# Window-attention and FFN layer on eight cores: transposing the attention matrix behind the V projection instead of ahead of it

## The chip, the cores and the metric

The kernel runs on the 8 cores of one Trainium2 chip. Every core computes 2 of the 16 sequences by itself, with all weights, and no core waits for another. The metric is the device time of the slowest core in microseconds (us).

## The reference

Attention here is over channels: for a window of 256 tokens and one head the 64 x 64 matrix q k^T (summed over the 256 tokens) goes through a softmax and is applied to v. Windows overlap by half (`step = 128`). Only the first 4096 rows of the joined windows are kept, which are those of windows 0 to 15 of a sequence.

```python
qkv = (xp @ W_qkv + b_qkv).reshape(B, Lp, 3, HEADS, HEAD_DIM)
...
attn = jnp.einsum('bhndw,bhnew->bhnde', qw, kw) * HEAD_DIM ** (-0.5)
attn = jax.nn.softmax(attn, axis=-1)
o = jnp.einsum('bhnde,bhnew->bhndw', attn, vw)
o = o.reshape(B, HEADS, -1, HEAD_DIM)
o = o.transpose(0, 2, 1, 3).reshape(B, -1, C)
o = o[:, :L]
return o @ W_out + b_out
...
x = _layernorm(x + attention(x)); x = _layernorm(x + ffn(x))
ffn(x) = (silu(x wg^T) * (x wu^T)) wd^T
```

Shapes: x 16 x 4096 x 1024, 16 heads of 64, hidden size 3072. The three FFN weights come as integers times 1/127.

## The kernel before

The program has two phases. Phase A does the attention and the first layer norm, and beside that turns and rescales the FFN weights. Phase B is the FFN with the second layer norm. The change touches phase A alone.

Phase A goes over the 2 sequences `s` and in each over 18 steps `t` (0 to 17). A step works on two windows that are one step apart, and on one block of 128 tokens. All of the order is that in which Python emits the code: each engine runs its instructions in that order, and there is no scheduler. A step of the middle (`t` from 2 to 16) emits, in this order:

- `prep_loads(2)` and `emit_xload(gt + 3)`: DMAs of two blocks of FFN weight and one block of x, issued by GpSimd.
- `emit_qkv_pass(0)` and `(1)`: TensorE multiplies the token block `x_fm` into q and k (18 matmuls of 512 columns each pass, lines 522 to 534, in `psum_qkv`), and VectorE copies the two halves out (lines 555 and 558).
- The first part of window n1 = t - 1: TensorE makes the 64 x 64 products of 16 heads in `psum_S` (line 587, 32 matmuls); VectorE takes the row maximum off (lines 599 and 605, `ssub`).
- The transposes of the softmax result of window n = t - 2: TensorE transposes `a_bd` into the first quarter of `psum_O` (lines 625 and 628, 16 of them), and VectorE copies that to `at_bf` (line 638).
- `emit_qkv_pass(2)`: v, in the same way, into `v_tmp`.
- `emit_xtr(gt + 2)`: the next x block transposed (8, line 287) and copied out (line 296).
- v transposed (8, line 662) and copied to `v_fm` (line 671).
- `flush_typf(which=1)`: the first normalised row block of the window before, `y_bf`, transposed (8, line 320) and copied out (line 334).
- The attention output: TensorE multiplies `v_fm` with `at_bf` into `psum_O` (line 693, 64 matmuls). It waits for the copy of line 638.
- `flush_typf(which=2)`: the second row block `y_bf`, the same.
- `prep_trs(2)`: two blocks of FFN weight (`w_in_bf`) are rescaled by VectorE (line 399), transposed by TensorE (line 413), copied to `wT_stage` (line 423) and stored by a DMA. In the last jobs (`wd`) a block has three such batches. There are 56 jobs, so the last steps of sequence 1 have none.
- The output projection: ScalarE copies the attention output to `attn_out` (line 781), TensorE multiplies it with `wout_bf` (lines 727 to 739, two row blocks), VectorE adds x from a DMA (`xr`, line 750, `y1pre`). ScalarE then does the exponential of window n1 (line 790) and the layer norm (lines 799 to 834), and VectorE the row sums and the block-diagonal form `a_bd` of window n1 (lines 843 to 865).

The transposes write to one of three banks in turn, `psum_TR`, `psum_S` and `psum_qkv`, given out by `claim_tr()`. Step t = 17 has no q, k and v and no new window: it only finishes the last one. In step 16 of sequence 1 `emit_wg_stream` issues one DMA of 6144 KB (`wgT`) on SyncE's queue, which also carries the `xr` loads.

Of the waits two matter here: the wait of the attention output for the copy, and VectorE's copy itself, which waits for its own last instruction as well:

```python
b.wait(v, "V", at_mm_done[gw])
b.wait(v, "V", b.tok("V"))
b.wait(v, "V", o_mm_done.get(gw - 1))
...
b.wait(t_, "T", atevac_done[gw])
b.wait(t_, "T", tv_done[s * TB + n])
b.wait(t_, "T", tv_done[s * TB + n + 1])
```

Of the kernel before, what the change touches and what calls it, by code (L numbers as in the profile page):

```python
# [9 lines left out]
BF16 = mybir.dt.bfloat16  # L10
# [10 lines left out]
TB = 17  # L21
NW = 16
# [38 lines left out]
def build_program(debug=False, seqs=SEQS, l=L):  # L61
    TB = l // 256 + 1
    NW = l // 256
# [30 lines left out]
    b = Bld(nc, es_outer)  # L94
# [14 lines left out]
    psum_O = PS("psum_O", [128, 2048], F32)  # L109
# [11 lines left out]
    ident_sb = SA("ident_sb", [128, 128], BF16)  # L121
# [16 lines left out]
    a_bd = SA("a_bd", [128, 2, 8, 128], BF16)  # L138
    at_bf = SA("at_bf", [128, 1024], BF16)
# [22 lines left out]
    with nc.Block() as blk:  # L162
        @blk.gpsimd
        def _(g):
            b.inc(g.memset(ones128[:, :], 1.0), "G", 1)
            b.inc(g.memset(ones1[:, :], 1.0), "G", 1)
            b.inc(g.memset(a_bd[:, :, :, :], 0.0), "G", 1)
            b.inc(g.memset(lneps[:, :], float(EPS)), "G", 1)
# [76 lines left out]
    s_mm_done, ssub_done, exp_done, scale_done, bd_done = {}, {}, {}, {}, {}  # L245
    at_mm_done, atevac_done, o_mm_done, oevac_done = {}, {}, {}, {}
    proj_done, resid_done, sq_done, apply_done = {}, {}, {}, {}
# [5 lines left out]
    with nc.Block() as blk:  # L253
# [52 lines left out]
        def emit_ty_one(gw, s, n, k2):  # L306
            wsl = n % 4
            if True:
                grt = s * RTS + 2 * n + k2
                rsl = grt % 2  # L310
                bk, qtok = claim_tr()
                bi, freetok = bk[0], bk[1]

                @blk.tensor
                def _(t_, grt=grt, rsl=rsl, bi=bi, freetok=freetok, qtok=qtok):
                    b.wait(t_, "T", apply_done[grt])
                    b.wait(t_, "T", freetok)
                    b.wait(t_, "T", qtok)
                    for c in range(8):
                        b.inc(t_.transpose(tr_slice(bi, 128 * c, 128 * (c + 1)),  # L320
                                           y1_bf[:, rsl, 128 * c:128 * (c + 1)],
                                           ident_sb[:, :]), "T", 1)
                tymm_done[grt] = b.tok("T")

                pp1 = pf_by_idx.get(pf_idx[0] - 1)
                pp2 = pf_by_idx.get(pf_idx[0] - 2)

                @blk.vector
                def _(v, grt=grt, rsl=rsl, k2=k2, wsl=wsl, bi=bi, pp1=pp1, pp2=pp2):
                    b.wait(v, "V", tymm_done[grt])  # L330
                    b.wait(v, "V", pp1)
                    b.wait(v, "V", pp2)
                    dst = y1fm_stage[:, wsl, :, 128 * k2:128 * (k2 + 1)]
                    b.inc(v.tensor_copy(dst, tr_slice(bi, 0, 1024)
                                        .rearrange("p (a b) -> p a b", a=8)),
                          "V", 1)
                ty_done[grt] = b.tok("V")
                bk[1] = ty_done[grt]

        def emit_pf(gw, s, n):  # L340
            wsl = n % 4
            nw0 = n - wsl
            pi = pf_idx[0]
            pf_idx[0] += 1
            prev2 = pf_by_idx.get(pi - 2)

            @blk.gpsimd
            def _(g, s=s, n=n, gw=gw, wsl=wsl, nw0=nw0, pi=pi, prev2=prev2):
                b.wait(g, "G", prev2)
                b.wait(g, "G", ty_done[s * RTS + 2 * n])  # L350
                b.wait(g, "G", ty_done[s * RTS + 2 * n + 1])
                src_ap = y1fm_stage[:, 0:wsl + 1, :, :].rearrange(
                    "p w a b -> p w (a b)")
                b.inc(g.dma_start(
                    y1fm_h.ap()[s, nw0:n + 1].rearrange(
                        "w p a b -> p w (a b)"),
                    src_ap), "pf%d" % (pi % 2), 16)
            pf_done[gw] = b.tok("pf%d" % (pi % 2))
            pf_by_idx[pi] = pf_done[gw]

        def flush_typf(which=2):
            if pending_typf[0] is not None:
                gw0, s0, n0 = pending_typf[0]
                if which >= 1 and pending_typf[0] not in ty_started:
                    ty_started.add(pending_typf[0])
                    emit_ty_one(gw0, s0, n0, 0)
                if which == 2:
                    emit_ty_one(gw0, s0, n0, 1)
                    if (n0 % 4 == 3) or (n0 == NW - 1):
                        emit_pf(gw0, s0, n0)  # L370
                    pending_typf[0] = None
# [124 lines left out]
        for s in range(SEQSv):  # L496
            for t in range(TB + 1):
# [5 lines left out]
                have_w2 = t >= 2  # L503
# [104 lines left out]
                    ssub_done[gw1] = b.tok("V")  # L608
                    tr_banks[1][1] = ssub_done[gw1]

                if have_w2:
                    n = t - 2
                    gw = s * NW + n
                    sl0 = (s * TB + n) % 3
                    sl1 = (s * TB + n + 1) % 3
                    wpar = gw % 2

                    @blk.tensor
                    def _(t_, gw=gw, wpar=wpar):
                        b.wait(t_, "T", bd_done[gw])  # L620
                        b.wait(t_, "T", oevac_done.get(gw - 1))
                        b.wait(t_, "T", resid_done.get(2 * (gw - 1)))
                        at_dst = psum_O[:, 0:512].bitcast(BF16)
                        for hp in range(8):
                            b.inc(t_.transpose(at_dst[0:64, 128 * hp:128 * (hp + 1)],
                                               a_bd[:, wpar, hp, 0:64], ident_sb[:, :]),
                                  "T", 1)
                            b.inc(t_.transpose(at_dst[64:128, 128 * hp:128 * (hp + 1)],
                                               a_bd[:, wpar, hp, 64:128], ident_sb[:, :]),
                                  "T", 1)  # L630
                    at_mm_done[gw] = b.tok("T")

                    @blk.vector
                    def _(v, gw=gw):
                        b.wait(v, "V", at_mm_done[gw])
                        b.wait(v, "V", b.tok("V"))
                        b.wait(v, "V", o_mm_done.get(gw - 1))
                        b.inc(v.tensor_copy(at_bf[:, :], psum_O[:, 0:512].bitcast(BF16)),
                              "V", 1)
                    atevac_done[gw] = b.tok("V")  # L640

                if have_qkv:
                    emit_qkv_pass(2)
                    qkv_free[0] = evac_half[((gt, 2), 1)]
# [29 lines left out]
                    vbk[1] = tv_done[gt]  # L674

                if have_w2:
                    flush_typf(which=1)

                    @blk.tensor
                    def _(t_, gw=gw, s=s, n=n, sl0=sl0, sl1=sl1):  # L680
# [248 lines left out]
    with nc.Block() as blk:  # L929
# [77 lines left out]
        for g in range(NGg):  # L1007
            s = g // (Lv // 256)
# [237 lines left out]
```

How the kernel before makes its waits and increments, by code:

```python
    def inc(self, instr, name, by=1):  # L40
        instr.then_inc(self.sems[name], by)
        self.cnt[name] += by
        return (name, self.cnt[name])
# [4 lines left out]
    def wait(self, eng, engkey, tok):  # L48
        if tok is None:
            return
        name, val = tok
        if val <= 0:
            return
        key = (engkey, name)
        if self.waited.get(key, 0) >= val:
            return
        self.waited[key] = val
        eng.wait_ge(self.sems[name], val)
# [1153 lines left out]
        @blk.gpsimd  # L1212
        def _(g_):
            g_.wait_ge(b.sems["st0"], b.cnt["st0"])
            g_.wait_ge(b.sems["st1"], b.cnt["st1"])
```

## Time and profile before

| | us |
|---|---|
| median of 3 runs | 3558.66 |
| lowest and highest of them | 3373.44, 3881.48 |
| the profiled execution | 3367.28 |
| its span on the slowest core (core 3) | 3365.7 |
| spans of the eight cores | 3352.1 to 3365.7 |
| TensorE busy in the span | 2947.0 (88%) |
| VectorE, ScalarE, GpSimd busy | 935.4, 1248.5, 182.8 |

The profiled execution is one run of the program with the hardware profiler on, and its span is the time from the first to the last instruction of its slowest core. The times of the rows are counted from the start of that span. A row of the timeline is: start, duration, engine, line of the source, operation, what is written from what, and in square brackets how long the engine had been idle and what ended that. PE is TensorE, DVE is VectorE, ACT is ScalarE, POOL is GpSimd, SP is SyncE. "PEclk" is the clock granted to TensorE as a share of 2.4 GHz, so 0.50 is 1.2 GHz.

### The profile page before, as it was taken

To read this page: it belongs to the slowest core of one execution; us is meant where nothing else is said; L and a number is where in the kernel's file an instruction comes from. 1 tells how busy PE (TensorE), PEld (TensorE's weight loads), DVE (VectorE), ACT (ScalarE), POOL (GpSimd) and SP (SyncE) were. 2 spreads that over 40 slices of the span, in tenths; PEclk is the share of its full clock that TensorE was granted. 3 is DMA by queue.
4 is the path that set the end of the run, shared out by engine and by line. 5 is a ranking of instruction groups with operands and counts; after the bars stand their busy time and mean duration, and the time that the engine had idled before them with its cause. 6 is when DMAs were issued, how large, how long until landed. Compare 5 with 4: busy or idle time off the path is not lost.

```text
span 3365.7 us, 61503 instructions; the slowest of 8 cores (3352.1 to 3365.7 us)
## 1 busy us (share of the span) xinstructions
PE 2947.0 (88%) x23572; PEld 1985.5 (59%) x23572; DVE 935.4 (28%) x1750; ACT 1248.5 (37%) x2721; POOL 182.8 (5%) x324
## 2 busy tenths in 40 slices
PE   0888888788866764999999999999999999999997
PEld 0344444344433432777777777777777777777775
DVE  0344444344434431112212212212212222222221
ACT  0245454525434443223333323323323323323333
POOL 1011111101111100000000000000000000000000
PEclk9999999899988886999999999999999999999998
DMA  7234434324444344401101101101101111101100
GB/s 124 50 99 132 123 107 121 110 85 110 122 129 119 113 139 146 132 32 51 45 32 51 45 32 51 45 32 51 45 32 51 45 33 50 45 35 48 45 32 26
DMA packets 77216, 245.71 MB, mean 73 GB/s; under 512 B 8576, under 2 KB 8576, under 8 KB 76928
## 3 DMA queue, kind: packets, MB, share of 16 engines
q0 software_dynamic: 43744, 138.96, 14.3%
q1 hardware_dynamic: 33184, 102.81, 9.2%
q8 instruction: 193, 3.16, 0.4%
q14 instruction: 95, 0.78, 0.1%
HBM read 175.16 MB, written 102.76 MB: 83 GB/s over the span
## 4 chain that ended last, share of the span: by engine, by line
PE 60%; ACT 0%; DMA 0%; DVE 0%; issue 0%; SPq 0%; POOL 0%; ACTq 0%; DVEq 0%; POOLq 0%
PE psum_qkv L1044 20%; PE psum_O L1025 10%; PE psum_S L1054 10%; PE psum_TR L1054 10%; PE psum_O L1029 10%; DMA wuT<-wuT_scr 0%; DVE y2pre L1099 0%; ACT y L1209 0%; ACT y2sq L1189 0%; ACT y2sq L1192 0%; SPq L989 0%; ACT L1189 0%; SPq L981 0%; DVE h_bf L1075 0%; ACT l2ln L1205 0%
## 5 line engine op out<-in xcount | busy, mean ns | idle before, releaser
L1044 PE MATMUL psum_qkv<-y1fm_sb,wgT 128*128 128x256 bf16 x6144 | 797.8, 273 | 19.6 <-DMA y1fm_sb<-y1fm_scr 19.6
L1044 PEld LDWEIGHTS psum_qkv<-y1fm_sb,wgT 128*128 128x128 bf16 x6144 | 601.8, 98 | 247.0 <-issue 19.8
L1139 ACT ACTIVATE sg_bf<-psum_qkv 128x256 bf16<-128x256 f32 x768 | 293.7, 382 | 1188.2 <-PE psum_S L1054 672.3
L1025 PE MATMUL psum_O<-wdT,h_bf 128*128 128x512 bf16 x1536 | 581.9, 379 | 0.6 <-DVE h_bf L1075 0.6
L1029 PE MATMUL psum_O<-wdT,h_bf 128*128 128x512 bf16 x1536 | 582.0, 379 | 0.0
L1054 PE MATMUL psum_S<-y1fm_sb,wuT 128*128 128x256 bf16 x3072 | 399.0, 273 | 6.8 <-DMA wuT<-wuT_scr 6.8
L1054 PE MATMUL psum_TR<-y1fm_sb,wuT 128*128 128x256 bf16 x3072 | 398.1, 273 | 0.0
L1075 DVE TENSOR_TENSOR h_bf<-psum_TR,sg_bf 128x256 bf16<-128x256 f32 x384 | 163.2, 425 | 794.3 <-PE psum_O L1025 675.1
L1075 DVE TENSOR_TENSOR h_bf<-psum_S,sg_bf 128x256 bf16<-128x256 f32 x384 | 163.2, 425 | 759.6 <-PE psum_O L1025 717.4
L522 PE MATMUL psum_qkv<-wqkv_bf,x_fm 128*128 128x512 bf16 x816 | 315.3, 386 | 48.5 <-DVE q_tm L555 43.4
L1054 PEld LDWEIGHTS psum_S<-y1fm_sb,wuT 128*128 128x128 bf16 x3072 | 300.8, 98 | 42.3 <-issue 7.3
L527 PE MATMUL psum_qkv<-wqkv_bf,x_fm 128*128 128x512 bf16 x816 | 314.7, 386 | 7.6 <-DVE q_tm L558 7.1
L1054 PEld LDWEIGHTS psum_TR<-y1fm_sb,wuT 128*128 128x128 bf16 x3072 | 300.6, 98 | 34.8
L727 PE MATMUL psum_O<-wout_bf,attn_out 128*128 128x512 bf16 x512 | 220.1, 430 | 8.4 <-ACT attn_out L781 8.4
L1025 PEld LDWEIGHTS psum_O<-wdT,h_bf 128*128 128x128 bf16 x1536 | 150.0, 98 | 119.8 <-issue 21.2
L732 PE MATMUL psum_O<-wout_bf,attn_out 128*128 128x512 bf16 x512 | 217.4, 425 | 0.5 <-ACT attn_out L781 0.5
L1029 PEld LDWEIGHTS psum_O<-wdT,h_bf 128*128 128x128 bf16 x1536 | 150.0, 98 | 98.8
L799 ACT ACTIVATE y1sq<-y1pre 128x1024 f32<-128x1024 f32 x64 | 67.6, 1057 | 301.6 <-DVE y1pre L750 298.4
L522 PEld LDWEIGHTS psum_qkv<-wqkv_bf,x_fm 128*128 128x128 bf16 x816 | 80.7, 99 | 155.9 <-issue 72.4
L527 PEld LDWEIGHTS psum_qkv<-wqkv_bf,x_fm 128*128 128x128 bf16 x816 | 80.9, 99 | 109.2 <-issue 24.4
L1126 POOL DMA_DIRECT2D out<-y x64 | 34.1, 533 | 2018.3 <-ACT y L1173 1860.2
L781 ACT ACT_TABLE_LOAD x32 | 41.1, 1283 | 252.0 <-PE psum_S L320 133.1
(145 smaller groups left out, 2424.1 us busy)
## 6 DMA issues: line engine op xcount, KB each, us to landing
xr<-x SPq DMA_DIRECT2D x64, 512.0 KB, 3.5
y1dbg<-y_f POOLq DMA_DIRECT2D x64, 512.0 KB, 3.0
y1r<-y1dbg SPq DMA_DIRECT2D x64, 512.0 KB, 4.2
out<-y POOLq DMA_DIRECT2D x64, 512.0 KB, 2.9
y1fm_scr<-y1fm_stage POOLq DMA_DIRECT2D x8, 2048.0 KB, 7.7
y1fm_sb<-y1fm_scr SPq DMA_DIRECT2D x32, 512.0 KB, 4.6
xt_bf<-x POOLq DMA_DIRECT2D x34, 256.0 KB, 7.7
wqkv_bf<-wqkv POOLq DMA_DIRECT2D x8, 768.0 KB, 27.9
```

The costliest lines, as they stand in the source:

```text
L522: b.inc(t_.matmul(psum_qkv[:, 0:512], lhsT, wqkv_bf[:, c, 1024 * p:1024 * p + 512], start=(c == 0), stop=False), "T", 1)
L527: b.inc(t_.matmul(psum_qkv[:, 512:1024], lhsT, wqkv_bf[:, c, 1024 * p + 512:1024 * (p + 1)], start=(c == 0), stop=False), "T", 1)
L727: b.inc(t_.matmul(pj[:, 0:512], lhsT, wout_bf[:, c, 0:512], start=(c == 0), stop=False, skip_group_check=True), "T", 1)
L732: b.inc(t_.matmul(pj[:, 512:1024], lhsT, wout_bf[:, c, 512:1024], start=(c == 0), stop=False, skip_group_check=True), "T", 1)
L781: b.inc(a.activation(attn_out[:, hp, rb:rb + 256] .rearrange("p (d c) -> p d c", c=4), psum_O[:, base:base + 256] .rearrange("p (c d) -> p ...
L799: b.inc(a.activation(y1sq[:, :], y1pre[:, rsl, :], AF.Identity, accum_out=sums[:, rsl, :]), "A", 1)
L1025: b.inc(t_.matmul(down_ps[:, 1024 * rs:1024 * rs + 512], lhsT, wdT[:, hc, 0:512], start=(hc == 0), stop=(hc == 23), skip_group_check=True) ...
L1029: b.inc(t_.matmul(down_ps[:, 1024 * rs + 512:1024 * (rs + 1)], lhsT, wdT[:, hc, 512:1024], start=(hc == 0), stop=(hc == 23), skip_group_ch ...
L1044: b.inc(t_.matmul(gate_ps[hsl], wgT[:, hc, 128 * dc:128 * (dc + 1)], y1fm_sb[:, gsl, dc, :], start=(dc == 0), stop=(dc == 7)), "T", 1)
L1054: b.inc(t_.matmul(up_ps[hsl], wuT[:, hc, 128 * dc:128 * (dc + 1)], y1fm_sb[:, gsl, dc, :], start=(dc == 0), stop=(dc == 7)), "T", 1)
L1075: b.inc(v.tensor_tensor(h_bf[:, hsl, :], up_ps[hsl], sg_bf[:, hsl, :], ALU.mult), "V", 1)
L1139: b.inc(a.activation(sg_bf[:, hsl, :], gate_ps[hsl], AF.Silu), "A", 1)
```

## The change

In every step the 16 transposes of `a_bd` and VectorE's copy to `at_bf` are emitted later: behind the v pass, the x transposes, the v transposes and the first `y_bf` transposes, right ahead of the attention output. Nothing is added or taken away; the waits are the same ones. In the source the blocks of v move up instead, which is the same order:

```diff
@@ -608,12 +608,48 @@
                     tr_banks[1][1] = ssub_done[gw1]
 
+                if have_qkv:
+                    emit_qkv_pass(2)
+                    qkv_free[0] = evac_half[((gt, 2), 1)]
+                    emit_xtr(gt + 2)
+
+                if s == SEQSv - 1 and t == TB - 1 and wprep_tr[0] >= 24:
+                    emit_wg_stream(gt)
+
+                if have_qkv:
+                    vbk, vqtok = claim_tr()
...
                 if have_w2:
                     n = t - 2
                     gw = s * NW + n
                     sl0 = (s * TB + n) % 3
                     sl1 = (s * TB + n + 1) % 3
                     wpar = gw % 2
+
+                    flush_typf(which=1)
 
                     @blk.tensor
                     def _(t_, gw=gw, wpar=wpar):
@@ -638,43 +674,6 @@
                     atevac_done[gw] = b.tok("V")
-
-                if have_qkv:
-                    emit_qkv_pass(2)
...
-                if have_w2:
-                    flush_typf(which=1)
 
                     @blk.tensor
                     def _(t_, gw=gw, s=s, n=n, sl0=sl0, sl1=sl1):
```

From line 608 on the line numbers change: the transposes are lines 661 and 664 (625 and 628 before), their copy is 674 (638), the v transposes are 631 (662) and their copy 640 (671), and what stands behind them is one line earlier (the attention output 692, the projection 726 and 731).

TensorE, step 3 of sequence 0, behind the q k products. Before:

```order
L576 UNCONDITIONAL_BRANCH
L587 MATMUL psum_S<-k_tm,q_tm 64x64 x32
L618 UNCONDITIONAL_BRANCH
L625 MATMUL psum_O<-ident_sb,a_bd 64x128
L628 MATMUL psum_O<-ident_sb,a_bd 64x128
```

After, the same place:

```order
L576 UNCONDITIONAL_BRANCH
L587 MATMUL psum_S<-k_tm,q_tm 64x64 x32
L515 UNCONDITIONAL_BRANCH
L522 MATMUL psum_qkv<-wqkv_bf,x_fm 128x512
L527 MATMUL psum_qkv<-wqkv_bf,x_fm 128x512
```

The v pass now follows the products at once. TensorE around the attention output (`psum_O<-at_bf,v_fm`), the same step. Before:

```order
L287 MATMUL psum_S<-ident_sb,xt_bf 128x128 x8
L654 UNCONDITIONAL_BRANCH
L662 MATMUL psum_qkv<-ident_sb,v_tmp 128x128 x8
L314 UNCONDITIONAL_BRANCH
L320 MATMUL psum_TR<-ident_sb,y_bf 128x128 x8
L679 UNCONDITIONAL_BRANCH
L693 MATMUL psum_O<-at_bf,v_fm 64x64 x64
```

After, what stands ahead of the attention output (the two rows of the transposes come eight times each; the last pair is shown):

```order
L661 MATMUL psum_O<-ident_sb,a_bd 64x128
L664 MATMUL psum_O<-ident_sb,a_bd 64x128
L678 UNCONDITIONAL_BRANCH
L692 MATMUL psum_O<-at_bf,v_fm 64x64 x64
L314 UNCONDITIONAL_BRANCH
L320 MATMUL psum_S<-ident_sb,y_bf 128x128 x8
```

The 16 transposes moved from behind the q k products to the place right ahead of the attention output. VectorE, the same step, from the row maximum to the second `y_bf` copy. Before:

```order
L599 TENSOR_REDUCE negmax<-psum_S 128x8
L605 TENSOR_TENSOR ssub<-psum_S,negmax 128x512
L633 UNCONDITIONAL_BRANCH
L638 COPY at_bf<-psum_O 128x1024
L542 UNCONDITIONAL_BRANCH
L555 CAST v_tmp<-psum_qkv 128x512
L558 CAST v_tmp<-psum_qkv 128x512
L292 UNCONDITIONAL_BRANCH
L296 COPY x_fm<-psum_S 128x1024
L667 UNCONDITIONAL_BRANCH
L671 COPY v_fm<-psum_qkv 128x1024
```

After, from the v copies on:

```order
L555 CAST v_tmp<-psum_qkv 128x512
L558 CAST v_tmp<-psum_qkv 128x512
L292 UNCONDITIONAL_BRANCH
L296 COPY x_fm<-psum_S 128x1024
L636 UNCONDITIONAL_BRANCH
L640 COPY v_fm<-psum_qkv 128x1024
L328 UNCONDITIONAL_BRANCH
L334 COPY y1fm_stage<-psum_TR 128x8x128
L669 UNCONDITIONAL_BRANCH
L674 COPY at_bf<-psum_O 128x1024
L328 UNCONDITIONAL_BRANCH
L334 COPY y1fm_stage<-psum_S 128x8x128
```

The copy to `at_bf` moved behind five other copies. ScalarE, GpSimd and SyncE keep their order.

## Rows read from the trace of the kernel before

**Rows 1.** The page, its head and the first row of part 1.

```profile
span 3365.7 us, 61503 instructions; the slowest of 8 cores (3352.1 to 3365.7 us)
...
PE 2947.0 (88%) x23572; PEld 1985.5 (59%) x23572; DVE 935.4 (28%) x1750; ACT 1248.5 (37%) x2721; POOL 182.8 (5%) x324
```

**Rows 2.** Windows, PE alone: stretch, length, busy, PEclk, DMA share, GB/s.

```profile
162.70:599.90 437.20, 354.99 (x3250) 0.96 0.40 117
330.30:364.20 33.90, 27.60 (x250) 0.95 0.36 102
364.20:396.40 32.20, 25.91 (x250) 1.00 0.39 107
...
1318.00:3365.00 2047.00, 2015.24 (x15360) 0.99 0.14 48
```

**Rows 3.** Timeline of one step (t = 2 of sequence 1), TensorE.

```profile
700.52 0.45 PE L587 MATMUL psum_S<-k_tm,q_tm 128*64 128x64 bf16 x16 [0.73 <-DVE k_tm L555]
...
701.79 0.22 PE L628 MATMUL psum_O<-ident_sb,a_bd 128*64 128x128 bf16 x1
...
705.41 0.38 PE L530 MATMUL psum_qkv<-bq_rep,ones 128*128 128x512 bf16 x1
...
707.55 0.61 PE L320 MATMUL psum_qkv<-ident_sb,y_bf 128*128 128x128 bf16 x8
...
708.09 1.52 PE L693 MATMUL psum_O<-at_bf,v_fm 128*64 128x64 bf16 x64
...
712.01 0.61 PE L413 MATMUL psum_S<-ident_sb,w_in_bf 128*128 128x128 bf16 x8 [1.84 <-DVE w_in_bf L399]
```

**Rows 4.** The same timeline, VectorE and ScalarE.

```profile
701.99 0.69 DVE L599 TENSOR_REDUCE negmax<-psum_S 128x8 f32<-128x512 f32 x1 [1.02 <-PE psum_O L628]
...
702.79 0.69 DVE L605 TENSOR_TENSOR ssub<-psum_S,negmax 128x512 f32<-128x512 f32 x1
...
703.58 0.69 DVE L638 COPY at_bf<-psum_O 128x1024 bf16<-128x1024 bf16 x1
...
705.89 0.69 DVE L555 CAST v_tmp<-psum_qkv 128x512 bf16<-128x512 f32 x1 [1.62 <-PE psum_qkv L530]
...
708.42 0.68 DVE L334 COPY y1fm_stage<-psum_qkv 128x1024 bf16<-128x1024 bf16 x1
...
710.54 1.28 ACT L781 ACT_TABLE_LOAD   x1 [24.58 <-PE psum_TR L320]
710.84 0.69 DVE L334 COPY y1fm_stage<-psum_TR 128x1024 bf16<-128x1024 bf16 x1 [1.73 <-PE psum_TR L320]
```

**Rows 5.** Timeline of the step ahead (t = 1, without `a_bd` transposes), TensorE.

```profile
680.99 0.45 PE L587 MATMUL psum_S<-k_tm,q_tm 128*64 128x64 bf16 x16 [0.73 <-DVE k_tm L555]
...
685.43 0.38 PE L530 MATMUL psum_qkv<-bq_rep,ones 128*128 128x512 bf16 x1
```

**Rows 6.** Timeline, TensorE and VectorE, where something other holds the step.

```profile
636.70 1.01 PE L320 MATMUL psum_qkv<-ident_sb,y_bf 128*128 128x128 bf16 x8 [4.79 <-ACT y_bf L834]
...
993.05 0.69 DVE L423 COPY wT_stage<-psum_qkv 128x1024 bf16<-128x1024 bf16 x1 [10.84 <-DMA wdT_scr<-wT_stage]
...
1041.46 0.69 DVE L423 COPY wT_stage<-psum_TR 128x1024 bf16<-128x1024 bf16 x1 [4.34 <-DMA wdT_scr<-wT_stage]
...
1252.76 2.55 DVE L750 TENSOR_TENSOR y1pre<-psum_O,xr 128x1024 f32<-128x1024 f32 x2 [19.89 <-DMA xr<-x]
...
1262.56 1.92 PE L693 MATMUL psum_O<-at_bf,v_fm 128*64 128x64 bf16 x64
```

**Rows 7.** Windows again, PE alone: two steps of sequence 1, and a pause.

```profile
801.20:833.20 32.00, 26.08 (x250) 1.00 0.40 108
934.20:968.70 34.50, 28.60 (x250) 0.90 0.43 115
...
978.00:986.00 8.00, 1.86 (x31) 1.00 1.02 213
```

More of the change, by code:

```diff
@@ L609, in build_program @@
                     tr_banks[1][1] = ssub_done[gw1]
-                if have_w2:
[L612 to L640, printed above, removed]
                 if have_qkv:
@@ L676, in build_program, with _ @@
                 if have_w2:
-                    flush_typf(which=1)
+                    n = t - 2
+                    gw = s * NW + n
+                    sl0 = (s * TB + n) % 3
+                    sl1 = (s * TB + n + 1) % 3
+                    wpar = gw % 2
+                    flush_typf(which=1)
+                    @blk.tensor
+                    def _(t_, gw=gw, wpar=wpar):
+                        b.wait(t_, "T", bd_done[gw])
+                        b.wait(t_, "T", oevac_done.get(gw - 1))
+                        b.wait(t_, "T", resid_done.get(2 * (gw - 1)))
+                        at_dst = psum_O[:, 0:512].bitcast(BF16)
+                        for hp in range(8):
+                            b.inc(t_.transpose(at_dst[0:64, 128 * hp:128 * (hp + 1)],
+                                               a_bd[:, wpar, hp, 0:64], ident_sb[:, :]),
+                                  "T", 1)
+                            b.inc(t_.transpose(at_dst[64:128, 128 * hp:128 * (hp + 1)],
+                                               a_bd[:, wpar, hp, 64:128], ident_sb[:, :]),
+                                  "T", 1)
+                    at_mm_done[gw] = b.tok("T")
+                    @blk.vector
+                    def _(v, gw=gw):
+                        b.wait(v, "V", at_mm_done[gw])
+                        b.wait(v, "V", b.tok("V"))
+                        b.wait(v, "V", o_mm_done.get(gw - 1))
+                        b.inc(v.tensor_copy(at_bf[:, :], psum_O[:, 0:512].bitcast(BF16)),
+                              "V", 1)
+                    atevac_done[gw] = b.tok("V")
                     @blk.tensor
```

## The prediction, made before the changed kernel was run

> **What bounds the kernel now.** I read the page first, then the windows, then the timeline of single steps. The page shows TensorE busy for 2947 of 3365.7 us and no other engine over 37% [rows 1]: TensorE's own instruction stream sets the time, and what counts is where that stream stands still. The windows split it. From 1318 us to the end (phase B) TensorE is busy for 2015 of 2047 us [rows 2], and the change doesn't touch that part. All that can move lies in the first 1318 us.
>
> There one step takes 32.0 to 34.5 us. The 13 steps from 162.7 to 599.9 us take 437.2 us, 33.6 each [rows 2]. Steps with the same work differ by the clock alone: 32.2 us with 1.00 granted all through, 33.9 us with a mean of 0.95 [rows 2]; in sequence 1 it is 32.0 us at 1.00 and 34.5 us at 0.90 [rows 7]. The clock falls to 1.2 GHz behind the thin stretch of a step, where TensorE has only transposes and waits for VectorE.
>
> Inside a step the timeline shows who waits for whom [rows 3, 4]. The q k products begin at 700.52, the 16 transposes in question end their issue at 701.79, the last part of the v pass starts at 705.41, the `y_bf` transposes at 707.55, and the attention output at 708.09 with no wait in front of it. Its partner, the copy to `at_bf` (703.58, 0.69 us), ran in a hole of VectorE: behind it VectorE was idle for 1.62 us. So today the round trip TensorE, VectorE, TensorE for `at_bf` is wholly covered by the v pass.
>
> **The change part by part.** Three things move in each step.
>
> (a) The transposes leave their old place. What follows, the v pass, starts earlier. With them the last part of the pass comes 705.41 - 700.52 = 4.89 us behind the start of the products, without them, in the step t = 1, 685.43 - 680.99 = 4.44 us [rows 3, 5]. Gain: 0.45 us. VectorE's chain of copies hangs on this point and shifts by the same.
>
> (b) At the new place TensorE needs those 0.45 us again. That would be a draw, if nothing waited.
>
> (c) The copy to `at_bf` is now on the path, and behind a queue. From 705.89 on VectorE makes five copies in a row without idle time (two halves of v, x, `v_fm`, first `y_bf`), of which the last runs from 708.42 to 709.10 [rows 4]. Shifted by (a) it ends at 708.65. The transposes follow the `y_bf` ones, issued from 707.10 to 707.64, and are through at about 708.3, before VectorE is free, so VectorE decides. The copy starts 0.11 us behind the end of its predecessor, since it waits for it to be complete (702.68 to 702.79 is such a pair [rows 4]), takes 0.69 us and ends at 709.45. TensorE starts some 0.15 us behind the end of a copy, which is an estimate from the 0.1 us between the end of line 530 and the start of line 555 [rows 3, 4]. The attention output starts at 709.60 instead of 708.09: 1.51 us late. Bounds: if the copy had to wait for nothing but the transposes, 708.3 + 0.1 + 0.69 + 0.15 = 709.24, 1.15 us late; if the five copies did not move up by 0.45 us, 1.96 us late. I take 1.51, since the chain without gaps is what the rows show.
>
> What stands behind the attention output follows it one by one: the table load and copies of ScalarE (710.54), the second `y_bf` transposes and their copy, with VectorE idle 1.73 us for them (710.84), the weight rescaling behind that copy in VectorE's order, and TensorE waiting 1.84 us for it (712.01) [rows 3, 4]. No row there shows slack towards something that doesn't move, so the whole 1.51 us goes to the projection and to the next step. VectorE has time for the move: what it does is the same, only in another order. The queues of GpSimd and SyncE keep their order, and each DMA is just issued with its step.
>
> How many steps pay? 30 steps have a v pass and transposes: t = 2 to 16, twice. Not all of them are set by TensorE.
> - Step 16 of sequence 1 waits 19.89 us for the x rows behind the large weight DMA [rows 6]; the delay disappears in that. It costs nothing.
> - The two steps t = 17 have no v pass. There the second `y_bf` transposes wait for ScalarE's layer norm (4.79 us [rows 6]), and ScalarE, which must also copy the attention output, is busy until then. Nothing.
> - Four steps handle `wd`. In the first, VectorE waits 10.84 us for a store that stands behind the loads of the weights, in the second 4.34 us [rows 6]; these loads are issued at the start of a step and don't move. I count 0 and 0.2 us for these, 1.1 and 1.5 for the other two: 2.8 us.
> - 25 steps remain: 25 x 1.51 = 37.8 us.
>
> Sum of the waits: 40.6 us. Bounds: 25 x 1.15 = 29 us, with none of the `wd` steps, and 29 x 1.96 = 57 us with all of them.
>
> (d) The clock. 22 of the steps (14 of sequence 0, 8 of sequence 1) are of the kind of which the windows tell. Today the clock costs them 33.6 - 32.2 = 1.4 us on the mean; a step with the short piece at 1.2 GHz pays 1.7 us, one with the long piece 34.5 - 32.0 = 2.5 us [rows 2, 7]. The thin stretch now has one more pause of about a microsecond and begins sooner. I can't work out from rows which step gets which piece; I expect the long one in about half of the steps and the short one in the others, less a few with none: 2.0 instead of 1.4 us, 22 x 0.6 = 13 us. Bounds: no piece at all, -1.4 x 22 = -31 us, and all long, +1.1 x 22 = +24 us. I take +13, nearer to the upper end, since the stretch only gets thinner.
>
> How TensorE's clock takes transposes shows in one pause. For 8 us in the first `wd` step TensorE had 1.86 us of work, all of it transposes (the second `y_bf` ones and three batches of weight), and the granted clock stayed at 1.00, that is 2.4 GHz [rows 7]. The change makes one run of 40 transposes out of 24 ahead of the attention output; by this row I count no fall of the clock for it. The Trainium skill, TensorE: Matmul & The Clock Gate, section "Part 4: PE-mode transpose", speaks against the change here: it says that transposes don't count as activity for the clock the way matmuls do. By that rule the clock would fall ahead of the attention output, which is what rival 2 does. The pause of rows 7 doesn't agree with it so far.
>
> **Sum.** 3367.3 + 40.6 + 13 = 3421 us, 1.6% more. The base is the profiled execution, 1.6 us over its own span; it lies 0.2% below the lowest of the three runs and 5.4% below their median, and the forecast is for an execution like the profiled one.
>
> **The rivals.**
> 1. The clock pays it back. The wait falls into a stretch in which the clock's pieces come and go, and a step that is 1.5 us longer may have them fall where TensorE pauses anyway. For it: steps without any piece exist, 32.2 and 32.0 us. Against it: they are few (the mean is 33.6), and a pause more has no way of raising the clock. 3367.3 + 40.6 - 31 = 3377 us, no difference that can be told.
> 2. The clock falls ahead of the attention output as well. Place: the run of 40 transposes and the pause in front of line 692. At 1.2 GHz the attention output took 1.92 instead of 1.52 us and eight transposes 1.01 instead of 0.61 [rows 3, 6]; with the transposes, the output and the second `y_bf` ones in it a step loses 1.2 us more. 22 x 1.2 = 26 us: 3447 us, 2.4% slower. It passes the limit of 2% when the clock falls there in over half of the steps. Against it stands the granted 1.00 of the pause in rows 7.
> 3. The wait is hidden. The new place changes nothing if the step's next part is held by something else, as the `wd` steps are. For it: the second copy to `wT_stage` and `y1pre` wait for stores in VectorE's queue. Against: TensorE waits for none of these in the steps of rows 3. With half of the wait hidden and the clock as now: 3367 + 20 = 3387 us.
> 4. The change doesn't do what it says, that is, TensorE has no new wait because VectorE reaches the copy in time. It would need VectorE idle in front of it, and rows 4 show five copies without a gap. It would give 3367 us.
>
> **How the numbers follow.** Forecast (3395 to 3440 us) 0.66; rival 1, 0.10; rival 2, 0.13; rival 3, 0.08; rival 4, 0.03. The range takes the forecast, rival 3 in part and rival 2: 3385 to 3450 us. 2% of 3367 is 67 us, and about that is what a measurement of this kernel can tell from no change; slower by more than that begins at 3435 us. Slower: rival 2 and the upper edge of the forecast, 0.17. Faster by over 2% has no mechanism: 0.01. The same: 0.82.
>
> **What would show it.** Right: TensorE's line 692 with some 1.3 us of idle time in front, ended by the copy of line 674, in some 28 steps, and that copy right behind line 334 on VectorE; line 530 of the v pass 4.44 us behind the start of the products; clean steps of 33.7 us where they were 32.2. Wrong: line 692 without a wait; the idle time in front of lines 726 or 413 shorter by what line 692 waits; a granted clock of 1.00 in most steps (rival 1), or 0.50 between lines 661 and 692 (rival 2); a phase B of another length.

## The result and the profile after

| | before | after |
|---|---|---|
| median of the runs | 3370.89 (10 runs) | 3427.37 (9 runs) |
| the profiled execution | 3367.28 | 3425.18 |
| its span, slowest core | 3365.7 (core 3) | 3423.6 (core 0) |
| TensorE busy | 2947.0 (88%) | 2971.4 (87%) |

The ratio of after to before is 1.0176, with a 95% interval of 1.0159 to 1.0193; runs in which the cores of a die were held at a lower clock count in the medians of the table, and are left out of this ratio and of all ratios below. The change makes the kernel 1.8% slower, clearly more than the measurement is uncertain. The forecast was 3421 us, in a range of 3385 to 3450 us, and called the two kernels "the same".

The head of the page after and its first row, and TensorE's busy share and granted clock over the 40 slices, answer to [rows 1]:

```profile
span 3423.6 us, 61504 instructions; the slowest of 8 cores (3405.9 to 3423.6 us)
...
PE 2971.4 (87%) x23572; PEld 1995.7 (58%) x23572; DVE 935.3 (27%) x1750; ACT 1247.8 (36%) x2721; POOL 182.8 (5%) x324
...
PE   1877787687875673899999999999999999999997
...
PEclk9999999899997896899999999999999999999998
```

VectorE's and ScalarE's busy times are those of before to 0.7 us, and so is the second phase: from its first matmul to the end it takes 2046.4 us before and 2047.3 us after on core 3. TensorE's busy time grew by 24 us with the same 23572 matmuls, which points to a lower clock.

The timeline of one step after, on core 0, answers to [rows 3, 4]. Columns as there.

```profile
730.15 0.45 PE L587 MATMUL psum_S<-k_tm,q_tm 128*64 128x64 bf16 x16 [0.73 <-DVE k_tm L555]
...
734.59 0.38 PE L530 MATMUL psum_qkv<-bq_rep,ones 128*128 128x512 bf16 x1
...
736.73 0.61 PE L320 MATMUL psum_qkv<-ident_sb,y_bf 128*128 128x128 bf16 x8
...
737.61 0.68 DVE L334 COPY y1fm_stage<-psum_qkv 128x1024 bf16<-128x1024 bf16 x1
...
738.39 0.69 DVE L674 COPY at_bf<-psum_O 128x1024 bf16<-128x1024 bf16 x1
739.23 1.49 PE L692 MATMUL psum_O<-at_bf,v_fm 128*64 128x64 bf16 x64 [1.32 <-DVE at_bf L674]
...
741.65 1.28 ACT L780 ACT_TABLE_LOAD   x1 [24.37 <-PE psum_TR L320]
741.95 0.69 DVE L334 COPY y1fm_stage<-psum_TR 128x1024 bf16<-128x1024 bf16 x1 [2.87 <-PE psum_TR L320]
...
743.12 0.61 PE L413 MATMUL psum_S<-ident_sb,w_in_bf 128*128 128x128 bf16 x8 [1.85 <-DVE w_in_bf L399]
```

Count from the start of the q k products. The last part of the v pass comes at 4.44 us (4.89 before). The first `y_bf` copy of VectorE ends at 8.14, the copy to `at_bf` starts at 8.24, and the attention output at 9.08, where it was 7.57: 1.51 us late. TensorE stood for 1.32 us in front of it, and VectorE waits 2.87 us for the second `y_bf` transposes instead of 1.73. The weight transposes behind it are late by about the same (12.97 instead of 11.49, 1.48 us). The list of waits of the first phase shows the new wait with its count; in the two steps t = 17 a wait for `y_bf` of up to 16.6 us now comes first, where before it was one for `a_bd` of up to 15.8.

```profile
PE psum_O L692 <- DVE at_bf L674: 41.7, 32, 1.5
...
PE psum_qkv L320 <- ACT y_bf L833: 19.1, 2, 16.6
```

Two steps in a row after, in windows on TensorE alone, and that part of the step of 730.15 us that runs from its x transposes to the end of its pause (stretch, length, busy, PEclk, DMA share, GB/s); they answer to [rows 2, 7]:

```profile
197.75:233.12 35.37, 27.74 (x251) 0.95 0.37 98
233.12:269.59 36.47, 28.84 (x251) 0.91 0.37 94
735.10:739.20 4.10, 2.31 (x41) 1.00 0.00 0
```

A "piece" is a stretch in which the granted clock is 0.50, that is 1.2 GHz, without a break. A step without a piece would be 33.7 us: 35.37 us less half of a piece of 3.4 us. The first of the two has such a piece, the second one of 6.8 us, and so they take turns. The third row is the run of 40 transposes and the pause: it kept its 2.4 GHz.

For the table below the step lengths were taken from the starts of the q k products on all eight cores, in each kernel: the 13 plain steps of sequence 0 (t = 3 to 15) and the 8 of sequence 1 (t = 2 to 9), the four steps with `wd`, and the time from the first q k products to the first matmul of the second phase; means over the cores, each from the one traced execution of a kernel. "Pieces" counts, of the 8 x 13 = 104 steps of sequence 0, those with any stretch at 1.2 GHz, and "long" those where one is over 6 us.

| kernel | 13 steps | 8 steps | 4 `wd` | first phase | pieces | long |
|---|---|---|---|---|---|---|
| before | 437.7 | 266.7 | 190.3 | 1204.1 | 89 | 2 |
| after | 465.6 | 283.9 | 193.8 | 1258.5 | 104 | 51 |
| e1 before, fill | 423.2 | 257.3 | 188.6 | 1172.1 | 6 | 1 |
| e2 after, fill | 441.4 | 269.0 | 193.0 | 1215.0 | 6 | 0 |
| e3 before, 7 busy | 466.0 | 283.7 | 192.2 | 1259.1 | 104 | 52 |
| e4 behind the v pass | 431.9 | 268.2 | 186.1 | 1192.5 | 75 | 19 |
| e5 after, copy twice | 487.1 | 295.3 | 196.9 | 1297.1 | 104 | 101 |
| e7 ahead of `y_bf` | 454.8 | 275.5 | 192.0 | 1235.4 | 104 | 25 |
| e8 e4 and fill | 418.2 | 254.2 | 189.5 | 1163.4 | 11 | 1 |
| e9 before, 11 busy | 483.6 | 287.0 | 194.8 | 1285.7 | 103 | 86 |
| e10 copy alone late | 475.9 | 289.5 | 197.6 | 1282.3 | 104 | 70 |
| e11 e1 once more | 424.1 | 257.0 | 188.2 | 1175.5 | 11 | 0 |

e1 and e11 are the same kernel, and their first phases differ by 3.4 us: so much two traced executions can be apart.

### The profile page after: what moved, and what is told of

Same layout as the page of the kernel before. It is cut to its first block, busy times and chain, and to the rows that moved or that the text cites. A ratio compares the mean times of both kernels' runs of the same rounds, so it can differ in the third digit from the quotient of the medians.

```text
span 3423.6 us, 61504 instructions; the slowest of 8 cores (3405.9 to 3423.6 us)
## 1 busy us (share of the span) xinstructions
PE 2971.4 (87%) x23572; PEld 1995.7 (58%) x23572; DVE 935.3 (27%) x1750; ACT 1247.8 (36%) x2721; POOL 182.8 (5%) x324
## 3 DMA queue, kind: packets, MB, share of 16 engines
q0 software_dynamic: 43744, 138.96, 14.9%
## 4 chain that ended last, share of the span: by engine, by line
PE 59%; ACT 0%; DMA 0%; DVE 0%; issue 0%; SPq 0%; POOL 0%; ACTq 0%; DVEq 0%; POOLq 0%
PE psum_qkv L1043 20%; PE psum_O L1024 10%; PE psum_S L1053 10%; PE psum_TR L1053 10%; PE psum_O L1028 10%; DMA wuT<-wuT_scr 0%; DVE y2pre L1098 0%; ACT y L1208 0%; ACT y2sq L1191 0%; ACT y2sq L1188 0%; SPq L988 0%; ACT L1188 0%; SPq L980 0%; DVE h_bf L1074 0%; ACT l2ln L1204 0%
## 5 line engine op out<-in xcount | busy, mean ns | idle before, releaser
L726 PE MATMUL psum_O<-wout_bf,attn_out 128*128 128x512 bf16 x512 | 225.9, 441 | 8.4 <-ACT attn_out L780 8.4
L731 PE MATMUL psum_O<-wout_bf,attn_out 128*128 128x512 bf16 x512 | 222.3, 434 | 0.5 <-ACT attn_out L780 0.5
```

Of the source, the lines that this page charges most:

```text
L726: b.inc(t_.matmul(pj[:, 0:512], lhsT, wout_bf[:, c, 0:512], start=(c == 0), stop=False, skip_group_check=True), "T", 1)
L731: b.inc(t_.matmul(pj[:, 512:1024], lhsT, wout_bf[:, c, 512:1024], start=(c == 0), stop=False, skip_group_check=True), "T", 1)
```

## The experiments

The theory was: the change puts VectorE's copy on the path, at the end of a row of five others, which costs 1.5 us in each of some 28 steps; and the longer step has more and longer pieces at 1.2 GHz. What had to be told apart: is it VectorE's queue or the place of the transposes on TensorE; how much is the wait, how much the clock; and does the clock follow the pause or the length of the step.

**Taking the clock out.** TensorE gets matmuls whose result is overwritten, in the two waits for the weight rescaling (about 1.8 and 1.35 us), in the kernel before (e1) and in the changed one (e2):

```diff
-                    b.wait(t_, "T", dq_tok)
...
                     b.wait(t_, "T", tr_free)
                     b.wait(t_, "T", qtok)
+                    if ib == 0:
+                        fdst = [psum_TR[:, :].bitcast(F32), psum_S[:, :],
+                                psum_qkv[:, 0:512]][bi]
+                        for k in range(8 if i % 2 == 0 else 6):
+                            b.inc(t_.matmul(fdst, ident_sb[:, :], wout_bf[:, k, 0:512],
+                                            start=True, stop=True), "T", 1)
+                    b.wait(t_, "T", dq_tok)
```

> The kernel before, with TensorE given throwaway matmuls (512 columns, into the bank that the weight transposes overwrite next) in the waits for VectorE's rescaling: 8 ahead of the first weight block of a step, 6 ahead of the second. The attention output is not held up by anything new. If the clock term is real and comes from the thin stretch: hardly any piece at 1.2 GHz in the 22 plain steps, these at 32.0 to 32.3 us each, and the kernel 25 to 35 us faster than before (0.990 to 0.993). If the clock doesn't hang on that stretch: the steps stay at 33.6 us on the mean and the time is that of before.

> The changed kernel with the same throwaway matmuls. Its distance to e1_before_fill is the wait alone, without the clock. Theory (wait of 1.51 us in 25 to 28 steps, plus a clock term of 13 to 18 us that the fill removes): 38 to 44 us above e1_before_fill, plain steps of 33.5 to 33.8 us without a piece at 1.2 GHz, near 3375 to 3390 us in all. Rival (the wait costs more than it shows, by late loads or stores): over 50 us above e1_before_fill.

Windows of a step of e1 (core 4) and of e2 (core 5), TensorE alone:

```profile
192.33:224.55 32.22, 28.94 (x265) 1.00 0.38 107
```

```profile
195.94:229.63 33.69, 29.09 (x265) 1.00 0.40 103
```

Both at a granted 1.00, and 33.69 - 32.22 = 1.47 us apart: that is the wait alone. e1 took 3337.2 us in its lowest run, some 30 us under before; its repetition, e11, with more runs gave a ratio:

> e1_before_fill once more, with more rounds, since it has no interval. Clock-term theory: 0.990 to 0.993 of before.

Measured 0.9921, 0.9905 to 0.9937. So the pieces at 1.2 GHz cost the kernel before some 27 us, and matmuls whose result nobody reads buy them back. They cost nothing themselves, because they stand where TensorE waits anyway: a step of e1 takes 32.22 us, a step of before without a piece 32.20 [rows 2]. e2 took 3379.5 us, 42 us above e1, as expected. Over the first phase, mean of the cores, e2 is 1215.0 - 1172.1 = 42.9 us above e1, and after is 1258.5 - 1204.1 = 54.4 us above before: 43 us are the wait, and the remaining 11.5 us the clock. With e11 in place of e1 the same sum gives 39.5 us and 14.9 us. So the wait is 40 to 43 us of the 54, and the clock 11 to 15.

**The same lateness with TensorE busy.** e3 puts 7 throwaway matmuls ahead of the attention output of the kernel before; e9 puts 11.

```diff
+                        for k in range(7):
+                            b.inc(t_.matmul(psum_O[:, 512:1024], ident_sb[:, :],
+                                            wout_bf[:, k, 0:512],
+                                            start=True, stop=True), "T", 1)
                         for hp in range(8):
```

> The kernel before, with 7 throwaway matmuls of 512 columns (7 x 0.216 = 1.51 us) right ahead of the attention output in every step: the output is as late as in the changed kernel, but TensorE is busy and not idle meanwhile. If the clock term comes from the length of the step (another place of the pieces in each step): the short and the long piece take turns as in the changed kernel and the time is its time within 6 us (ratio 1.015 to 1.019). If it comes from the new pause itself (a thinner stretch): no long pieces, steps of 35.1 to 35.4 us with the short piece, ratio 1.011 to 1.014.

Two steps in a row of e3, core 1:

```profile
199.57:234.89 35.32, 29.07 (x258) 0.95 0.35 98
234.89:271.31 36.42, 30.13 (x257) 0.91 0.35 94
```

Measured 1.0165 (1.0145 to 1.0185): the same lengths, the same turns of clock and the same count of long pieces (52 against 51) as in the changed kernel, without its pause. At this size the clock term follows the length of the step, not the idle time at this place. That speaks against my reason for it ("the stretch only gets thinner"). Length alone doesn't make the pieces either: the steps of e2 are as long, 33.69 us, and with the waits for the rescaling filled only 6 of 104 have one.

**More of the wait.** e5 does the copy to `at_bf` twice in the changed kernel, e6 in the kernel before.

```diff
+                        b.inc(v.tensor_copy(at_bf[:, :], psum_O[:, 0:512].bitcast(BF16)),
+                              "V", 1)
+                        b.wait(v, "V", b.tok("V"))
                         b.inc(v.tensor_copy(at_bf[:, :], psum_O[:, 0:512].bitcast(BF16)),
                               "V", 1)
```

> The changed kernel with VectorE's copy to at_bf done twice in a row, so the attention output waits 0.80 us longer (2.31 us in all). Both theories expect 0.80 us more wait in some 28 steps. Additive theory: the clock term stays as in the changed kernel, so 22 us above it, near 3449 us (ratio to before 1.024). Rhythm theory (the clock term hangs on how long a step is, not on how long the pause is): with clean steps of 34.5 us the turns of short and long piece change to mostly single short pieces in sequence 0, the clock term falls there, and the kernel is only 6 to 16 us above the changed one, 3433 to 3443 us (1.019 to 1.022).

Measured 1.0288 (1.0259 to 1.0316), over both theories. The timeline of one step of e5 (core 2) shows the new pause, and windows around it the clock:

```profile
209.32 1.53 PE L695 MATMUL psum_O<-at_bf,v_fm 128*64 128x64 bf16 x64 [2.12 <-DVE at_bf L677]
210.79 1.03 PE L320 MATMUL psum_S<-ident_sb,y_bf 128*128 128x128 bf16 x8
```

```profile
204.60:209.30 4.70, 1.73 (x34) 1.00 0.98 154
209.30:211.30 2.00, 1.98 (x70) 0.76 0.19 37
211.30:219.50 8.20, 5.24 (x28) 0.50 0.08 32
```

Ahead of the attention output TensorE had 4.7 us with transposes and a pause of 2.12 us only, and the clock fell to 1.2 GHz a microsecond into the output, at 210.32, and stayed there for 10.2 us. In 101 of 104 steps one of these long pieces came; in the changed kernel, with 1.32 us of pause, none began ahead of the weight transposes. This is rival 2 of the prediction, at a pause 0.8 us longer than the change makes, and with the fall a microsecond behind the pause instead of in it. e9 has the attention output as late as in e5 (10.17 and 10.10 us behind the start of the q k products), with TensorE busy in the place of the pause; its transposes stand at the old place:

> As e3_before_busy, with 11 throwaway matmuls (11 x 0.216 = 2.37 us) ahead of the attention output: a step as long as in e5_after_twice (clean 34.5), but TensorE busy instead of waiting. Length theory (only the length of a step decides which pieces at 1.2 GHz it gets): the 10.2 us pieces of e5_after_twice in nearly every step, time within 6 us of it (ratio 1.027 to 1.031). Pause theory (past some point it is the idle time itself): pieces of 3.4 and 6.8 us only, ratio 1.020 to 1.026.

One step of e9, core 7:

```profile
237.61:275.07 37.46, 31.16 (x261) 0.91 0.36 92
```

Measured 1.0238 (1.0218 to 1.0259): pieces of 6.8 us, none of 10.2, and 11 us less in the first phase than e5. So the pause theory holds past this point: the longer step brings the 6.8 us pieces (86 of 104 steps), and the idle pause the 10.2 us ones.

> The kernel before with the same copy twice, at its old place. VectorE has 1.62 us idle there, and the second copy takes 0.80. Theory (the old place is a hole, the copy is free): time of before, 0.998 to 1.002, step lengths of 32.2 and 33.9 us unchanged. Rival (VectorE's time counts anywhere): 0.8 us in 30 steps, 24 us slower, 1.007.

Measured 1.0001 (0.9989 to 1.0013). VectorE on core 5 in a step of e6:

```profile
225.34 0.69 DVE L638 COPY at_bf<-psum_O 128x1024 bf16<-128x1024 bf16 x1
226.13 0.69 DVE L641 COPY at_bf<-psum_O 128x1024 bf16<-128x1024 bf16 x1
227.65 0.69 DVE L555 CAST v_tmp<-psum_qkv 128x512 bf16<-128x512 f32 x1 [0.82 <-PE psum_qkv L530]
```

The second copy took 0.8 of the 1.6 us of idle time, nothing else moved. The same extra copy cost nothing here and 1.1% in e5: what it costs is set by its place.

**Other places.** e10 moves VectorE's copy alone; TensorE keeps the order of before.

> Only VectorE's copy to at_bf moved behind the first y_bf copy; TensorE's order is that of before. VectorE's queue theory: the chain of five copies is not moved up by 0.45 us, so the attention output starts 1.96 us late, clean steps of 34.1 to 34.2 us in sequence 0, more wait in total than in the changed kernel (28 x 1.96 = 55 us), and in all at least as slow as it (1.017 to 1.028). Rival (it is the transposes' place on TensorE that costs): under half of the change's loss, below 1.009.

Measured 1.0232 (1.0210 to 1.0254), more than the whole change. The wait in e10 (core 5), and in e7 (core 0):

```profile
PE psum_O L694 <- DVE at_bf L675: 60.4, 32, 2.1
```

```profile
PE psum_O L692 <- DVE at_bf L672: 19.3, 30, 1.2
```

So it is VectorE's queue; TensorE's part of the change even helps, since it lets the chain of copies start 0.45 us sooner. The pause of 1.9 us also brought the 10.2 us pieces, in 60 of the 104 steps. e10 and e9 have the same order on TensorE but for the 11 matmuls, so it isn't the transposes' new place that brings them.

> The transposes and the at_bf copy behind the v transposes but ahead of the first y_bf transposes: the copy is fifth in VectorE's row and not sixth. By the chain of copies the attention output starts 0.9 us late instead of 1.5: clean steps of 33.1 us (sequence 0) and 32.9 us (sequence 1). 28 x 0.92 = 26 us of wait. Rhythm theory: at this length nearly only short pieces, clock term -5 to 0 us, so 20 to 27 us slower than before (1.006 to 1.008). Additive theory (clock term in proportion to the wait): 34 us slower (1.010).

Measured 1.0094 (1.0076 to 1.0112), above the rhythm theory's numbers and just below the additive one; the interval reaches both, so this run doesn't decide between them. One place further up in VectorE's row takes away 0.6 us per step. The long pieces didn't go away as I had worked out from the step lengths; 25 steps still had one.

> The transposes and the copy to at_bf put behind the v pass but ahead of the x transposes. The copy is third in VectorE's row instead of sixth, so the attention output should have no wait. Theory: no wait at the attention output, and the transposes fill part of the time in which TensorE waits for the v copies, so 0 to 0.45 us per step less: 0 to 15 us faster than before (0.995 to 1.000). Rival (it is the order on TensorE that costs, any place behind the v pass is bad): 20 us or more slower than before.

e4 emits the block right behind `emit_qkv_pass(2)`. VectorE and TensorE of one step (core 0), and then that step in windows with the one ahead of it:

```profile
271.23 0.68 DVE L558 CAST v_tmp<-psum_qkv 128x512 bf16<-128x512 f32 x1
272.01 0.69 DVE L642 COPY at_bf<-psum_O 128x1024 bf16<-128x1024 bf16 x1
...
272.06 0.61 PE L664 MATMUL psum_qkv<-ident_sb,v_tmp 128*128 128x128 bf16 x8 [0.20 <-DVE v_tmp L558]
...
273.04 1.52 PE L695 MATMUL psum_O<-at_bf,v_fm 128*64 128x64 bf16 x64
```

```profile
231.34:265.70 34.36, 28.31 (x248) 0.90 0.36 100
265.70:297.46 31.76, 25.88 (x248) 1.00 0.56 175
```

No wait at line 695, and the clean step is 31.76 us, 0.45 less than before: the transposes now fill time in which TensorE waited for the v copies. Measured 0.9992 (0.9978 to 1.0005), no difference. The mean core gained 11.6 us in the first phase, but the step beside it shows where part of it goes: more long pieces (19 against 2), and not on all cores alike. The spans run from 3328.8 to 3358.8 us, and the slowest core counts. With the fill the gain must come out:

> e4_behind_v with the throwaway matmuls of e1_before_fill. If its 0.45 us per step are real and only the pieces at 1.2 GHz hid them, it must be 0.45 x 28 = 13 us faster than e1_before_fill: clean steps of 31.5 to 31.8 us, about 3324 us, 0.987 of before. Rival (the gain is lost for another reason than the clock): no faster than e1_before_fill.

One step of e8, core 1:

```profile
192.61:224.37 31.76, 29.16 (x264) 1.00 0.39 109
```

Measured 0.9878 (0.9861 to 0.9895), median 3326.6 us. Of the 13 us expected against e1, 9 to 11 came (first phase 1163.4 against 1172.1; 3326.6 against 3337.2 us); against e11 it is 12 us in the first phase, and the intervals of the two ratios don't touch. e8 beats both kernels: 40 us faster than before and 101 us faster than after.

## Why the prediction was right or wrong

- **The gain (a), 0.45 us:** right, 4.44 us to the last part of the v pass. e10, which goes without it, is slower than the change.
- **The lateness (c), 1.51 us:** right to the hundredth, by the chain of copies in VectorE's order. Neither bound was met; e10, with the transposes at their old place, shows the upper one: its output comes 9.75 us behind the start of the q k products in a step of sequence 0 where it was 7.79, which is 1.96 us late.
- **No slack behind it:** right. e2 against e1 gives 1.47 us per plain step.
- **How many steps pay:** the sum of the waits was 40.6 us and is 39.5 to 42.9 (e2 against e11 and e1). The wait itself stands in 32 steps, not in some 28: in the two steps t = 17 it is there as well, and hidden, as forecast. The four `wd` steps were sized at 2.8 us. They gave 3.5 on the mean of the cores, clock included, and 4.4 to 4.8 with the fill, but by single steps and cores between -3.1 and +3.8 us: their waits for DMAs don't follow the order alone, and that part I can't explain further.
- **The clock (d):** 13 us forecast, 11 to 15 measured. The half and half of long and short pieces came (51 and 53 of 104). The reason that I gave for it was wrong: the stretch doesn't have to get thinner, a step longer by the same with TensorE busy has the same pieces (e3). The half was a guess without a row behind it, so that this term came out is luck.
- **Rival 1** fell: no step of the 104 was without a piece. **Rivals 3 and 4** fell with e2 and with the row of line 692. **Rival 2** fell for this change, with 1.00 granted over the 40 transposes and the pause; something like it comes true at a pause of 1.9 to 2.1 us (e10, e5), and the prediction had not tied it to the length of the pause.
- **The row against rival 2** was cut short. The prediction took the granted 1.00 from 978 to 986 us as a sign that the clock stands such a stretch. The next window of the same trace, and the row that ends the pause:

```profile
984.00:986.00 2.00, 0.00 (x0) 1.00 0.95 274
986.00:988.00 2.00, 0.00 (x0) 0.64 1.03 417
...
998.94 1.01 PE L413 MATMUL psum_S<-ident_sb,w_in_bf 128*128 128x128 bf16 x8 [16.70 <-DVE w_in_bf L399]
```

  TensorE stood idle for 16.70 us there, 982.2 to 998.9, and 986 lies inside. The clock fell at 986.55 and stayed at 1.2 GHz for 17.1 us. So that row was weak evidence: it shows that 8 us with only transposes and idle time can pass at 2.4 GHz, and also that the clock falls right behind.
- The Trainium skill's rule on transposes in TensorE: Matmul & The Clock Gate, "Part 4: PE-mode transpose", is not refuted by any of this: in e5 the clock did fall behind a stretch of transposes and a pause, and no run here tells the transposes' share from the pause's.
- **The step that failed** is the last one, "about that is what a measurement of this kernel can tell from no change". I took 2% for the resolution and so put 0.82 on "the same" beside a sum of +1.6%. The runs showed 1.0176 with an interval of 0.17% to either side, 1.0159 to 1.0193, and the kernel is slower beyond doubt. Each term of the sum said slower; the class should have said it too. In us the sum is 6 us (0.2%) under the median, and its two terms, 40.6 and 13 us, lie within what the runs show for them.

## What to carry to other kernels

Moving a short block costs what the round trip at its new place costs, and this is read from the row of the engine that answers: count the copies queued ahead of it, each with its duration, and see whether the asking engine has other work meanwhile. Here a copy in a hole was free, even twice; the same copy at the end of a busy row was paid in full. Look also at what a longer step does to TensorE's clock, and fill waits for VectorE with throwaway matmuls where the bank is free anyway: it gave 0.8% here, and it lets other small gains reach the end.

## What the runs showed of the hardware

- The granted clock turned by itself into a pattern. With clean steps of 33.7 us, pieces of 3.4 and 6.8 us took turns through all of sequence 0 (53 and 51 of 104 steps), whether TensorE was idle (after) or busy (e3) in the added 1.5 us; with 32.2 us it was one short piece in 87 steps, and 2 long ones. With the two waits for the rescaling filled, steps of 33.69 us had a piece in 6 of 104 (e2).
- With 4.7 us of nothing but transposes and idle time, the last 2.12 us idle, the clock fell from 2.4 to 1.2 GHz 1.0 us into the matmuls that followed, for 10.2 us (e5); with 1.32 us of pause it stayed at 2.4 GHz there (after). In the kernel before, one stretch of 8.5 us with only transposes and idle time passed at 2.4 GHz before the clock fell, so the length of a pause doesn't settle it alone.
- 14 matmuls a step whose results nobody reads took some 27 us off the kernel (e11, 0.9921); of 104 steps 11 had a piece at 1.2 GHz where it had been 89.
